# Shift rows of a head pair move from a bank of the exponentials to a bank of the maxima, in windowed attention on one Trainium2 core

## The reference

```python
# local attention (L0_attn_b), window 128, scores masked outside the band
scores = jnp.einsum('blhd,bmhd->bhlm', q, k) * scale + bias
attn = jax.nn.softmax(scores, axis=-1)
ctx = jnp.einsum('bhlm,bmhd->blhd', attn, v).reshape(B, L, D)
# sliding attention (L1_attn_a), window 64, by blocks
scores = jnp.where(valid[None, None], scores, -1000000000.0)
p = jax.nn.softmax(scores.reshape(B, Hn, nb, BS, nw1 * BS), axis=-1)
out = jnp.einsum('bhnqwk,bhnwkd->bhnqd', p, vg)
```

## Time and profile before

| what | value |
|---|---|
| three timed runs | 2485.8, 2488.71, 2491.26 us; median 2488.71 |
| the profiled execution | 2493.88 us, of which the span is 2492.2 us |
| granted TensorE clock, mean over the span | 0.891 of full speed |
| busy over the span | PE 2091.5 us (84%), DVE 1805.5 (72%), ACT 1612.9 (65%), POOL 517.8 (21%) |
| DVE line 1728, both stages, 512 reductions | 179.9 us, 420 ns each |
| PE line 1532, both stages, 512 matmuls | 52.0 us, 286 ns each, 78.7 us of idle time ahead of them |
| ACT line 1692, both stages, 128 exponentials | 114.4 us, 917 ns each, 77.6 us of idle time ahead of them |

### The profile page before, as it was taken

The page is one execution under the profiler, slowest core; times in us unless marked ns, Lnnn a source line. Parts: engine busy times, 40 slices in busy tenths (PEclk is TensorE's granted clock), DMA queues, the critical chain, the costliest instruction groups (busy, mean ns, idle before and its releaser), DMA issues. The chain is left out here.

```text
span 2492.2 us, 43833 instructions
## 1 busy us (share of the span) xinstructions
PE 2091.5 (84%) x15400; PEld 902.9 (36%) x15400; DVE 1805.5 (72%) x4863; ACT 1612.9 (65%) x2354; POOL 517.8 (21%) x798
## 2 busy tenths in 40 slices
PE   6487388769367799999999987947999999999696
PEld 2365145657245222222222236721222222222375
DVE  7733595443676889999999925368999999996543
ACT  3033355334345479999999963424999999999343
POOL 6165131147111000000000005720000000000075
PEclk8588599879689689999999988955999999999798
DMA  2312560211480510111111021116011011010213
GB/s 67 95 45 74 76 119 16 78 51 51 84 145 18 146 27 20 26 31 25 21 30 28 4 75 34 51 38 156 16 30 31 16 30 30 16 30 2 74 48 87
DMA packets 94696, 127.15 MB, mean 51 GB/s; under 512 B 20906, under 2 KB 72592, under 8 KB 94480
## 3 DMA queue, kind: packets, MB, share of 16 engines
q1 hardware_dynamic: 82832, 102.99, 19.0%
q0 software_dynamic: 11648, 21.36, 3.0%
HBM read 79.88 MB, written 42.40 MB: 49 GB/s over the span
## 5 line engine op out<-in xcount | busy, mean ns | idle before, releaser
L1323 ACT ACTIVATE prob<-ps 128x1024 f32<-128x1024 f32 x1024 | 989.7, 1023 | 43.1 <-PE ps L1207 23.1
L1376 DVE TENSOR_REDUCE pair_mx<-ps 128x1 f32<-128x512 f32 x1520 | 960.2, 684 | 73.8 <-PE ps L1176 72.2
L1176 PE MATMUL ps<-k_stack,q_stack 48*128 48x512 bf16 x2048 | 591.9, 402 | 28.9 <-PEq L928 9.1
L1221 PE MATMUL ps<-prob,v_head 128*32 128x512 f32 x4096 | 547.6, 607 | 1.1 <-ACT prob L1323 1.0
L1207 PE MATMUL ps<-q_stack,k_stack 51*128 51x512 bf16 x2048 | 450.8, 384 | 6.4 <-ACT prob L1323 3.8
L1176 PEld LDWEIGHTS ps<-k_stack,q_stack 48*128 48x128 bf16 x2048 | 153.2, 94 | 496.6 <-DVE pair_mx L1376 346.8
L2258 DVE TENSOR_TENSOR hid<-silu,ps 128x256 f32<-128x256 f32 (+1 forms) x190 | 87.9, 463 | 249.2 <-PE ps L2111 169.7
L1207 PEld LDWEIGHTS ps<-q_stack,k_stack 51*128 51x128 bf16 x2048 | 103.1, 93 | 302.4 <-ACT prob L1323 269.9
L1728 DVE CUSTOM_DVE_ANT_0 ps<-ps,mask 128x256 f32<-128x256 f32 (+2 forms) x512 | 179.9, 420 | 42.0 <-PE ps L1532 39.7
L1297 ACT ACTIVATE qk<-ps 128x512 f32<-128x512 f32 x264 | 157.6, 597 | 58.3 <-PE ps L1176 48.5
L2111 PE MATMUL ps<-weight_raw,block 128*128 x632 | 193.5, 430 | 0.0
(11 more groups left out here) (249 smaller groups left out, 2260.0 us busy)
## 6 DMA issues: line engine op xcount, KB each, us to landing
q_stack<-image_dram SPq DMA_DIRECT2D x88, 192.0 KB, 4.6
k_stack<-k_wide_dram SPq DMA_DIRECT2D x60, 240.0 KB, 5.3
arena<-e_rows SPq DMA_DIRECT2D x32, 256.0 KB, 4.9
k_stack<-image_dram SPq DMA_DIRECT2D x32, 192.0 KB, 4.5
image_dram<-parts SPq DMA_DIRECT2D x28, 192.0 KB, 5.1
k_wide_dram<-parts SPq DMA_DIRECT2D x2, 1800.0 KB, 17.3
image_dram<-parts SPq DMA_DIRECT2D x28, 128.0 KB, 5.1
weight_raw<-in_L_ffn_Wg_dram SPq DMA_DIRECT2D x6, 528.0 KB, 5.0
```

The source lines that it names most:

```text
L1176: nc.tensor.matmul(max_bank(n), rows_of(c.q_stack, b, g, ROWS, slice(t * P, (t + 1) * P)), rows_of(c.k_rows, b, g, ROWS, slice(k * CHUNK, ...
L1221: ins = nc.tensor.matmul(out, c.v_head[:, e % 2, kb, :], unit, start=(kb == 0 and e % 2 == 0), stop=(kb == TILES - 1 and e % 2 == 1), skip ...
L1323: nc.scalar.activation(c.prob[:, u % P_UNITS, :], c.ps[:, 2 * (u % 2) * CHUNK:2 * (u % 2) * CHUNK + UNIT], ACT.Exp, scale=scale).then_inc( ...
L1376: ins = nc.vector.reduce_max(mx[:, w:w + 1], max_bank(n), AX.X)
```

## The change

The rows get a number of their own in `place`, at step 2 of the next pair's loop, ahead of that step's scores (`rows_at`, `ROWS_AT` = 2), and with it one of the banks 4 to 6. A new helper, `wait_bank`, waits for what used the bank three numbers before: for ACT's copy (`rows_taken`) where that was a set of rows, otherwise for DVE's count, in which rows no longer have a share (`taken_through`). `max_units` calls it for each of its two banks, ahead of its first matmul. The waits for the exponentials around the rows go, as does the semaphore `rows_ready`: ACT and POOL wait for the rows by `max_ready`. ACT's copy keeps its place ahead of unit 5 (`ROWS_UNIT`).

```diff
-    SHIFT_UNIT = 5
+    ROWS_UNIT = 5
...
-    SHIFT_BANK = 2 * ((SHIFT_UNIT + 1) % 2)
+    ROWS_AT = 2
...
+    def rows_at(e):
+
+        return (e + 1, ROWS_AT)
...
                 if turn_at(e) == (h, w):
                     place["turn", e] = len(place)
+                if rows_at(e) == (h, w):
+                    place["rows", e] = len(place)
...
+    unit_at = {n: key for key, n in place.items()}
+    taken_through = []
+    for n in range(len(place)):
+        taken_through.append((taken_through[-1] if n else 0) + (unit_at[n][0] != "rows"))
...
+    def wait_bank(pe, n):
+
+        last = n - len(MAX_BANKS)
+        if last < 0:
+            return
+        if unit_at[last][0] == "rows":
+            pe.wait_ge(*rows_taken.after(unit_at[last][1] + 1))
+        else:
+            pe.wait_ge(*max_taken.after(taken_through[last]))
...
-        last = place[h, w, 1]
-        if last >= len(MAX_BANKS):
-            pe.wait_ge(*max_taken.after(last - len(MAX_BANKS) + 1))
+        for g in range(2):
+            wait_bank(pe, place[h, w, g])
...
     def shift_rows(pe, e):
 
+        n = place["rows", e]
+        wait_bank(pe, n)
         pe.wait_ge(*split.after((e + 1) * SPLIT_OPS))
-        if e:
-            pe.wait_ge(*exp_done.after((e - 1) * EXP_UNITS + SHIFT_UNIT))
-        nc.tensor.matmul(bank(c, SHIFT_BANK)[0:2 * PARTS * TILES, 0:P], shift, c.ident16[:], start=True, stop=True)\
-            .then_inc(rows_ready.sem, 1)
+        nc.tensor.matmul(bank(c, max_bank(n))[0:2 * PARTS * TILES, 0:P], shift, c.ident16[:], start=True, stop=True)\
+            .then_inc(max_ready.sem, 1)
...
-        if u == SHIFT_UNIT and e < PAIRS - 1:
-            shift_rows(pe, e + 1)
-        if u == SHIFT_UNIT + 1 and e < PAIRS - 1:
-            pe.wait_ge(*rows_taken.after(e + 2))
...
+                    if h and rows_at(h - 1) == (h, w):
+                        shift_rows(pe, h - 1)
                     max_units(pe, h, w)
-                    if h == 1 and w == 2:
-                        shift_rows(pe, 0)
-                        pe.wait_ge(*rows_taken.after(1))
```

More of the change, by code:

```diff
@@ L1450, in window_heads_stage @@
     split = c.count("full_shift_split")
-    rows_ready = c.count("full_shift_rows_ready")
     rows_taken = c.count("full_shift_rows_taken")
@@ L1539, in turn @@
         n = place["turn", e]
-        pe.wait_ge(*max_taken.after(n - len(MAX_BANKS) + 1))
+        wait_bank(pe, n)
         pe.wait_ge(*out_taken.after(e + 1))
@@ L1651, in _ @@
                     turn(pe, PAIRS - 3)
+                if rows_at(PAIRS - 1) == (PAIRS, at - STEP):
+                    shift_rows(pe, PAIRS - 1)
                 catch_up(PAIRS - 2, at)
@@ L1669, in take_rows @@
             def take_rows(e):
-                act.wait_ge(*rows_ready.after(e + 1))
+                n = place["rows", e]
+                act.wait_ge(*max_ready.after(n + 1))
                 if e:
@@ L1674, in take_rows @@
                         act.wait_ge(*shift_loaded[g].after(e * 16))
-                nc.scalar.activation(c.pair_rows[:], bank(c, SHIFT_BANK)[0:2 * PARTS * TILES, 0:P], ACT.Copy).then_inc(rows_taken.sem, 1)
+                nc.scalar.activation(c.pair_rows[:], bank(c, max_bank(n))[0:2 * PARTS * TILES, 0:P], ACT.Copy).then_inc(rows_taken.sem, 1)
             if kept:
@@ L1683, in _ @@
                         take_out(e - 1)
-                    if u == SHIFT_UNIT and e < PAIRS - 1:
+                    if u == ROWS_UNIT and e < PAIRS - 1:
                         take_rows(e + 1)
@@ L1702, in take_turned @@
                 if e:
-                    dve.wait_ge(*max_taken.after(place["turn", e - 1] + 1))
+                    dve.wait_ge(*max_taken.after(taken_through[place["turn", e - 1]]))
                 for g in range(2):
@@ L1730, in _ @@
                         ins.then_inc(max_taken.sem, 1)
-                dve.wait_ge(*max_taken.after(place[h, STEP - 1, 1] + 1))
+                dve.wait_ge(*max_taken.after(taken_through[place[h, STEP - 1, 1]]))
                 if h:
@@ L1759, in split_shift @@
                 if h:
-                    pool.wait_ge(*rows_ready.after(h))
+                    pool.wait_ge(*max_ready.after(place["rows", h - 1] + 1))
                 at = h * SPLIT_OPS
@@ L1817, in window_heads_stage @@
     pass_first(c, True)
-    for sig, n in ((v_staged, 2 * PAIRS), (max_ready, len(place)), (max_taken, len(place)), (rowmax_ready, PAIRS),
-                   (split, PAIRS * SPLIT_OPS), (rows_ready, PAIRS), (rows_taken, PAIRS), (shift_loaded[0], PAIRS * 16),
+    for sig, n in ((v_staged, 2 * PAIRS), (max_ready, len(place)), (max_taken, taken_through[-1]), (rowmax_ready, PAIRS),
+                   (split, PAIRS * SPLIT_OPS), (rows_taken, PAIRS), (shift_loaded[0], PAIRS * 16),
                    (shift_loaded[1], PAIRS * 16), (st_ready, PAIRS * EXP_UNITS), (exp_done, PAIRS * EXP_UNITS),
```

## The result

The kernel after takes 2500.76 us (median of 10 runs, 2495.1 to 2505.4), the kernel before 2490.78 us on the same chip (10 runs, 2485.8 to 2498.2). The ratio is 1.0035, with a 95% interval of 1.0023 to 1.0046: **8.7 us slower**, between 5.7 and 11.5. The forecast was 6.8 us slower; by the ratio the median that the prediction started from, 2488.7, would become 2497.4 us, against 2495.5.

What follows compares the result with a forecast made beforehand. PE and DVE, both nearly full, were taken to bound the attention stages, handing work through three banks. Terms of 6.2 + 1.4 - 0.8 gave +6.8 us on the median 2488.7, so 2495.5 us, range 2488 to 2502.

Steps and rivals of the forecast that it cites:

- Part 1: Loops 2 to 7, scores of step 2: one more bank place delays PE 0.77 and 0.63 us; net +6.2 us.
- the freed slot: The rows' matmul leaves its place behind line 1602, giving back 0.19 us per loop in the first stage, 0.18 in the second.
- the 0.37 us at step 3: DVE's wait for PE's scores at step 3: PE is late there, so no slack absorbs the delay.
- Rival B: DVE catches up where PE stands still in other steps, each loop regaining half: +3.7 us, 2492.4 us; chance 0.17.
- Part 4: Second wait in `max_units`, 62 times in each stage: between nothing and 7.4 us, taken as 0.
- rival C: The second wait has its upper price: +6.8 + 7.4, at most 2503 us, more likely half, 2499; chance 0.08.
- Parts 2 and 3: Loop 1 and pair 0's rows, +1.4 us; small gains around the rows, -0.8 us.
- Part 2: Loop 1, PE's step 2: later by 0.77 us and, in the second stage, 0.63, with no slot saved; +1.4 us.
- The negation's 1.20 us: DVE's line 1734, covered by POOL's second bias addition: earlier POOL work no longer meets it, gain taken as 0.24 us.
- The wait of pair 7's rows: At the stage's end these rows waited 0.20 us for an exponential's bank, twice over the two stages; gone, 0.40 us.
- The other small terms: Among them, pair 0's exponentials in the second stage no longer wait 0.18 us for the rows' transfer.
- Rival D: TensorE's clock falls behind each longer hole at step 2: 1.3 us a loop, 16 us, 2511 us; chance 0.03.

## Why the prediction was right, and where it wasn't

- **What bounds the loop.** PE and DVE hand each other work through three banks: right. I then counted on PE's side, which gave the bank's price rightly; where the time goes showed on DVE's side.
- **Part 1, the bank.** Right, in place, releaser and size: 0.77 and 0.63 forecast, 0.76 and 0.63 measured alone; with the freed slot 0.58 and 0.45 forecast, 0.58 and 0.45 measured. That nothing is made up was right too: the 0.37 us at step 3 stayed. Rival B (half given back) is refuted.
- **Part 4, the second wait.** This is the term that was mis-sized: taken as 0, it is 0.27 us in a loop, 3.5 us in all by its own run, about half its stated upper end of 7.4. The reason given for 0 fails: line 1551 has two waits but PE arrives there late, and a late arrival hides the price, which shows only where PE stands and waits. The row I needed was in the trace of before: at step 0, where that kernel already has two waits, PE waits 0.40 us, at steps 4 and 6 0.31. So rival C is real at half its price, as its own text took to be likelier, beside the forecast and not instead of it. That the total still fell into the stated range is the range's width and not this term's merit.
- **Parts 2 and 3.** Part 2 shows in the distance from the scores of step 2 in loop 0 to those in loop 1: its mean over the eight profiles with one more place at step 2 lies 0.79 and 0.69 us above that of the six without (first and second stage), for 0.77 and 0.63 forecast. The negation's 1.20 us is gone, at 0.18 everywhere. The wait of pair 7's rows is gone: the turns of pairs 5 and 6 stand 12.65 us apart where they stood 12.90, 0.25 for the 0.20 forecast (first stage). The other small terms, all under 1 us, lie below what these runs separate.
- **The sum.** 6.8 forecast, 8.7 measured (5.7 to 11.5): 9.3 by the loops 2 to 7, 6.1 for the bank and 3.2 for the waits. The two stages whole grew by 9.1 in the execution without falls, so what Parts 2 and 3 cover, and loop 2, which has no turn, come out near nothing together, where 0.6 was forecast.
- **Rival D.** The clock does fall behind the longer holes, at 1.1 to 1.6 us a fall where I had put 1.3, but behind one in ten and not behind each. The sign named for it, a granted clock under 1.00 between 340 and 400 us, was there in the first profile of the kernel after and not in the second. The section of the Trainium skill's page "TensorE: Matmul & The Clock Gate" that the prediction named is borne out in kind, since the granted clock swung between the two levels among these waits (1.00, then a mean of 0.78 over 4 us); most holes of 1.38 us passed without it.

## What to carry to other kernels

Before a shared bank gets one more user, look at who stands waiting for that rotation, and write down which engine then runs dry: here DVE, which stood still for 0.48 us in each loop of the first stage for that reason alone. A second semaphore wait isn't free where its engine is the one that stands still; wait once, for the later of two counts, where the later one implies the earlier. And where an engine must wait, put ahead of the wait the work that would otherwise delay the next hand-over: that made both kernels 5 us faster, while filler gave nothing.

## What the runs showed of the hardware

- A second wait on PE's queue is an instruction of 51 ns, and lets a standing PE go 0.09 us later (0.40 instead of 0.31 us, 0.88 instead of 0.79; three places of a loop).
- The granted clock fell behind a hole of 1.0 to 1.6 us in some loops only, 4 of 40, and a fall cost 1.1 to 1.6 us. Two profiles of one kernel had two such falls and none.
